# Cross-attention: the products with the values, from one head at a time on 128 output rows to four heads side by side on 32 rows each, a group of four heads in one go

## The reference, cut to what matters

```
q = (x @ Wq).reshape(b, n, 32, 16)            # b = 4 batches, n = 512 queries, 32 heads of 16
k, v = jnp.split(ctx @ Wkv, 2, axis=-1)       # 512 keys
q, k = apply_axial_rope(q, pos), apply_axial_rope(k, pos)
logits = jnp.einsum('bqhd,bkhd->bhqk', q, k) * scale
w = jax.nn.softmax(logits, axis=-1)
attn = jnp.einsum('bhqk,bkhd->bqhd', w, v)
return attn.reshape(b, n, 512) @ Wout + bout
```

## Time and profile before

| | |
|---|---|
| median of 3 runs | 6926.31 us (6921.14 to 6929.72) |
| profiled execution | 6916.92 us, its span 6915.1 us |
| first score matmul of the stage | 5753.1 us from the span's start |
| last copy out of `out_ps` begins | 6535.2 us |
| PE, DVE, ACT, POOL busy over the span | 82%, 62%, 40%, 25% |

### The profile page before, as it was taken

One profiled execution on the slowest core, in us unless ns is written; L12 is line 12 of the kernel. 1 busy time (PEld: TensorE's weight loads), 2 busy tenths in 40 slices (PEclk: granted clock), 3 DMA queues, 4 the chain that ended last, 5 costly groups with the idle time before them and its releaser, 6 DMA issues. The chain is left out here.

```text
span 6915.1 us, 91344 instructions
## 1 busy us (share of the span) xinstructions
PE 5668.5 (82%) x29317; PEld 3875.2 (56%) x29317; DVE 4276.0 (62%) x7058; ACT 2762.2 (40%) x5087; POOL 1762.9 (25%) x1756
## 2 busy tenths in 40 slices
PE   4889338996788888888888888888888777999946
PEld 3656225563466666666666666666666534555523
DVE  4777663223377777777667677767776445666566
ACT  4555111110244444444444444444444224666512
POOL 2556000202133333333333333333333141000100
PEclk8999659998799999999999999999999898999978
DMA  1011004344200001000001100000000021111110
GB/s 53 25 25 25 18 18 185 125 153 142 86 28 26 26 26 35 26 26 26 26 26 40 29 24 28 26 26 24 27 26 22 1 75 61 44 43 43 34 50 24
DMA packets 261461, 307.07 MB, mean 44 GB/s; under 512 B 27840, under 2 KB 180928, under 8 KB 259808
## 3 DMA queue, kind: packets, MB, share of 16 engines
q1 hardware_dynamic: 247120, 248.43, 11.8%
q0 software_dynamic: 13984, 54.01, 2.2%
HBM read 245.88 MB, written 56.49 MB: 44 GB/s over the span
## 5 line engine op out<-in xcount | busy, mean ns | idle before, releaser
L1647 POOL TENSOR_TENSOR delta_rule_suffix<-delta_rule_suffix,delta_rule_prefix 128x256 f32<-128x256 f32 x448 | 496.2, 1108 | 1780.3 <-ACT delta_rule_prefix L1703 1174.8
L1956 PE MATMUL delta_rule_level<-delta_rule_qk_second,delta_rule_k_first 128*128 128x128 f32 x3072 | 427.1, 283 | 142.8 <-DVE delta_rule_L_large L1768 126.0
L1956 PEld LDWEIGHTS delta_rule_level<-delta_rule_qk_second,delta_rule_k_first 128*128 128x128 f32 x3072 | 385.6, 195 | 193.9 <-DVE delta_rule_qk_second L1776 142.0
L2398 PE MATMUL attend_out_ps<-attend_probsT,attend_v_head 128*128 128x512 f32 x1024 | 481.5, 593 | 0.0
L1929 PE MATMUL delta_rule_proj<-delta_rule_hT,delta_rule_w_qkv 128*128 128x512 f32 x1024 | 474.4, 607 | 0.0
L1638 POOL TENSOR_TENSOR delta_rule_k_first<-delta_rule_qk,delta_rule_suffix 128x256 f32<-128x256 f32 x384 | 306.4, 798 | 627.8 <-PE delta_rule_level L1944 494.4
L2425 DVE TENSOR_REDUCE attend_top<-attend_scores 128x1 f32<-128x512 f32 x512 | 328.5, 684 | 159.2 <-PE attend_scores L2380 159.1
L472 DVE TENSOR_TENSOR_SCAN scan_hs<-scan_decay,scan_inp 128x512 f32<-128x512 f32 x256 | 307.9, 1216 | 189.6 <-PE scan_inp L534 91.3
L309 POOL TENSOR_TENSOR scan_hc<-scan_hs,scan_c_rows 128x512 f32<-128x512 f32 x256 | 333.1, 1308 | 272.5 <-DVE scan_hs L472 253.3
L1864 DVE TENSOR_TENSOR delta_rule_X<-delta_rule_X,delta_rule_inv 128x512 f32<-128x512 f32 x384 | 262.3, 683 | 199.8 <-PE delta_rule_inv L1985 199.8
L1776 DVE TENSOR_TENSOR delta_rule_qk_second<-delta_rule_qk,delta_rule_prefix 128x512 f32<-128x512 f32 x448 | 339.9, 759 | 48.8 <-issue 14.0
(11 more groups left out here) (466 smaller groups left out, 12893.7 us busy)
## 6 DMA issues: line engine op xcount, KB each, us to landing
moe_w_d<-in_w_down SPq DMA_DIRECT2D x39, 512.0 KB, 4.3
scan_c_rows<-bc_dram SPq DMA_DIRECT2D x64, 256.0 KB, 3.7
delta_rule_w_qkv<-in_kda_wq SPq DMA_DIRECT2D x64, 256.0 KB
delta_rule_w_qkv<-in_kda_wk SPq DMA_DIRECT2D x64, 256.0 KB
delta_rule_w_qkv<-in_kda_wv SPq DMA_DIRECT2D x64, 256.0 KB
delta_rule_inv_beta<-beta_dram SPq DMA_DIRECT2D x64, 256.0 KB
delta_rule_w_o<-in_kda_wo SPq DMA_DIRECT2D x64, 256.0 KB, 4.5
parts_dram<-qkv_parts POOLq DMA_DIRECT2D x24, 512.0 KB, 6.1
```

The source lines that it names most:

```text
L1647: pool.tensor_tensor(first, first, whole_second, ALU.mult).then_inc(suffix_done, 1)
L1956: last = pe.matmul(level_ps[(i + 1) % 2][:, c, :], left, qk_second[:, i % 2, :, c * CHUNK // 2:(c + 1) * CHUNK // 2], start=True, stop=True)
L2398: last = pe.matmul(out_ps[:], v_head[:, j, i, :], probsT[:, j % 2, i, :], start=(j == 0 and i == 0), stop=(j == H - 1 and i == TPB - 1))
```

## The change

The eight heads of a tile form two halves (GROUP = 4), half 0 for steps j = 0 to 3 and half 1 for steps 4 to 7. `head(j)` says which head step j works on: 0, 2, 4, 6 in the first half and 1, 3, 5, 7 in the second. The stationary operand `v_head[:, j, i, :]` is now 32 columns wide (COLS), 16 with values and 16 zeros, and the output of head q of a half goes to rows 32q to 32q + 31 of `out_ps`. The two halves add up in the same rows. `probsT` keeps all eight heads instead of two, 64 KB a partition instead of 16 KB. `v_head` shrinks from 16 KB to 4 KB a partition.

The products of a half are issued in one run of 16 program matmuls, i = 0 to 3 outside and q = 0 to 3 inside, between turn 1 and turn 2 of one head step: of step 5 for half 0 of the same tile, of step 1 for half 1 of the tile before. Their number is the same as before, 512, and the moving operand is still 128x512. The last half stands bare at the end. `weighed` counts halves now. DVE and ACT wait for it ahead of the first write to a `probsT` slot; DVE's copy of `out_ps` moves from step 0 to step 3.

```
+    GROUP = 4
+    WEIGH_AT = 1
+    COLS = 2 * X_DIM
+    def head(j):
+        return 2 * (j % GROUP) + j // GROUP
...
-        v_head = sc.sb("v_head", [P, H, TPB, P])
+        v_head = sc.sb("v_head", [P, H, TPB, COLS])
-        probsT = sc.sb("probsT", [P, 2, TPB, S])
+        probsT = sc.sb("probsT", [P, H, TPB, S])
...
-                def weigh(n, j, i):
-                    m = n * H + j
+                def weigh(n, half, i):
+                    m = n * H + half * GROUP + GROUP - 1
                     pe.wait_ge((even_copied, odd_copied)[i % 2], 2 * m + i // 2 + 1)
                     if i == 0:
                         pe.wait_ge(v_ready, m + 1)
-                        if j == 0:
+                        if half == 0:
                             pe.wait_ge(out_copied, n)
-                    last = pe.matmul(out_ps[:], v_head[:, j, i, :], probsT[:, j % 2, i, :],
-                                     start=(j == 0 and i == 0), stop=(j == H - 1 and i == TPB - 1))
+                    for q in range(GROUP):
+                        j = half * GROUP + q
+                        last = pe.matmul(out_ps[q * COLS:(q + 1) * COLS, :], v_head[:, j, i, :], probsT[:, j, i, :],
+                                         start=(half == 0 and i == 0), stop=(half == 1 and i == TPB - 1))
...
                     for i in range(TPB):
                         turn(n, j, i)
-                        if i % 2 == 1 and not first:
-                            weigh(*before, i - 1)
-                            weigh(*before, i)
+                        if i == WEIGH_AT and j % GROUP == 1:
+                            for part in range(TPB):
+                                if j >= GROUP:
+                                    weigh(n, 0, part)
+                                elif not first_tile:
+                                    weigh(n - 1, 1, part)
                     if last:
                         for i in range(TPB):
-                            weigh(n, j, i)
+                            weigh(n, 1, i)
...
                         if i % 2 == 1:
                             dve.wait_ge(probs_turned, TPB * m + i + 1)
-                            dve.tensor_copy(probsT[:, j % 2, i, :], turned[1][:].rearrange("p a b -> p (a b)")).then_inc(odd_copied, 1)
+                            if i == 1:
+                                dve.wait_ge(weighed, 2 * n + j // GROUP + 1)
+                            dve.tensor_copy(probsT[:, j, i, :], turned[1][:].rearrange("p a b -> p (a b)")).then_inc(odd_copied, 1)
...
-                    if j == 0 and not first:
+                    if j == GROUP - 1 and not first_tile:
                         copy_out(n - 1)
```

More of the change, by code:

```diff
@@ L2326, in steps @@
             for j in range(H):
-                step(0, j, j == 0, False)
+                step(0, j, j == 0, False, True)
             with engine.Fori(1, N - 1) as n:
                 for j in range(H):
-                    step(n, j, False, False)
+                    step(n, j, False, False, False)
             for j in range(H):
-                step(N - 1, j, False, j == H - 1)
+                step(N - 1, j, False, j == H - 1, False)
         with nc.Block() as block:
@@ L2339, in _ @@
                 sp.sem_inc(exp_done, TPB)
-                sp.sem_inc(weighed, H)
+                sp.sem_inc(weighed, 2)
                 sp.sem_inc(sums_copied, 2)
@@ L2345, in _ @@
                         s = j % RING
-                        at = slice(j * X_DIM, (j + 1) * X_DIM)
+                        at = slice(head(j) * X_DIM, (head(j) + 1) * X_DIM)
                         sp.wait_ge(scores_done, TPB * (n * H + j + 1))
@@ L2365, in _ @@
                     for j in range(H):
-                        at = slice(j * X_DIM, (j + 1) * X_DIM)
-                        pool.wait_ge(weighed, n * H + j + 1)
-                        pool.tensor_copy(v_head[:, j, :, at], v_flat[:, n, :, at]).then_inc(v_ready, 1)
+                        at = slice(head(j) * X_DIM, (head(j) + 1) * X_DIM)
+                        to = slice(j // GROUP * X_DIM, (j // GROUP + 1) * X_DIM)
+                        pool.wait_ge(weighed, n * 2 + j // GROUP + 1)
+                        pool.tensor_copy(v_head[:, j, :, to], v_flat[:, n, :, at]).then_inc(v_ready, 1)
                 pool.wait_ge(bout_loaded, 16)
@@ L2395, in weigh, with step @@
                         pe.wait_ge(v_ready, m + 1)
-                        if j == 0:
+                        if half == 0:
                             pe.wait_ge(out_copied, n)
-                    last = pe.matmul(out_ps[:], v_head[:, j, i, :], probsT[:, j % 2, i, :],
-                                     start=(j == 0 and i == 0), stop=(j == H - 1 and i == TPB - 1))
+                    for q in range(GROUP):
+                        j = half * GROUP + q
+                        last = pe.matmul(out_ps[q * COLS:(q + 1) * COLS, :], v_head[:, j, i, :], probsT[:, j, i, :],
+                                         start=(half == 0 and i == 0), stop=(half == 1 and i == TPB - 1))
                     if i == TPB - 1:
                         last.then_inc(weighed, 1)
-                def step(n, j, first, last):
-                    before = (n, j - 1) if j else (n - 1, H - 1)
+                def step(n, j, first, last, first_tile):
                     if first:
@@ L2427, in copy_out, with step @@
                 def copy_out(n):
-                    dve.wait_ge(weighed, H + (n + 1) * H)
+                    dve.wait_ge(weighed, 2 + (n + 1) * 2)
                     dve.tensor_copy(out_flat[:, n, :], out_ps[:]).then_inc(out_copied, 1)
-                def step(n, j, first, last):
+                def step(n, j, first, last, first_tile):
                     m = n * H + j
@@ L2467, in step @@
                             act.wait_ge(probs_turned, TPB * m + i + 1)
-                            act.activation(probsT[:, j % 2, i, :], turned[0][:].rearrange("p a b -> p (a b)"),
+                            if i == 0:
+                                act.wait_ge(weighed, 2 * n + j // GROUP + 1)
+                            act.activation(probsT[:, j, i, :], turned[0][:].rearrange("p a b -> p (a b)"),
                                            ACT.Copy).then_inc(even_copied, 1)
```

2 lines of the change are left out of this document (1 added, 1 removed).

## The result

The changed kernel takes 6844.18 us (median of 4 runs, 6840.94 to 6848.36) against 6926.35 (4 runs, 6921.14 to 6929.72) for the kernel before: a ratio of 0.9887, 95% interval 0.9874 to 0.9899. That is 82.2 us less (the interval allows 70 to 87), where 48 more was forecast.

What follows compares the result with a forecast made beforehand. The prediction took a full PE to bound the stage, 6.04 us a head, 773 us. Head steps 602, bursts 208, last burst 7.7 and start 3 made 821, so 48 more: 6974 us, range 6840 to 7025.

Steps and rivals of the forecast that it cites:

- W: Length of one burst of 16 program matmuls on PE, taken as 7.7 us with only neighbouring strips overlapping.
- The narrow and wide rows: Profile rows of the kernel before where 16-column records stand 0.43 us apart on their own strip, between wide matmuls.
- the rival: All four strips run at once, burst 3.6 us, the SP queue then decides: 6843 us, chance 0.25.
- the bounds of 3.6 and 14.0: Limits on the burst's length in us: all four strips at once, or no overlap.
- The cap: SP queue's transfers allow no lasting head rate under 5.39 us, so the change gives at most 83 us.
- A head step without products, 4.7: Closed chain of ACT and PE for one head when no products are issued, taken as 4.7 us.
- The delay, W - 1.0: Time a burst between turn 1 and turn 2 adds to the chain: 1.0 us hidden, 6.7 added.
- the forecast's own sum: Stage time from head steps 602, bursts inside steps 208, last burst 7.7 and start 3: 821 us against 773.
- Break-even at W of about 6.2: Burst length in us at which the changed kernel would take as long as the kernel before.
- The edits costed at nothing: DVE's moved copy of `out_ps`, the two added waits on `weighed` and POOL's copies were to cost nothing.
- The sign that the prediction gave for the queue: In steps without a burst, ACT's even copies 5.4 us apart with SP never waiting would mean the queue bounds them.
- The clock's rival: PE, no longer full, loses its full granted clock for part of the time: 46 us more, 7020 us, chance 0.08.

Runs made afterwards that it cites:

- s9: Changed kernel, cross-attention layer alone, with key loads moved to GpSimd's queue and GpSimd's 16 additions spread one to a tile: 1044.01 us.
- The wide burst: Changed kernel, cross-attention layer alone, products regrouped but kept on 128 output columns instead of narrow strips: 1372.75 us.
- s11: Kernel before the change, cross-attention layer alone, with key loads moved from SP's to GpSimd's queue: 1149.57 us.
- s2: Changed kernel with the five other phases left out, cross-attention layer alone: 1057.95 us.
- s10: Changed kernel, cross-attention layer alone, with products spread over four steps, key loads on GpSimd's queue and additions one to a tile: 980.17 us.
- f12: Whole changed kernel, all phases, with spread products, key loads on GpSimd and additions one to a tile: 6760.86 us, ratio 0.9771 to the kernel before.
- s7: Changed kernel, cross-attention layer alone, with key loads moved to GpSimd's queue, the 16 additions still in one piece: 1062.55 us.
- s8: Changed kernel, cross-attention layer alone, with products spread over four steps and key loads on GpSimd's queue, additions in one piece: 982.64 us.

## Why the prediction was wrong

**The step that failed** is W, the length of the burst, 7.7 us in the sum and 3.57 in the trace. The step is in the part on the burst: "If matmuls start in program order, strip 1's first starts beside strip 0's second, not before it. So only neighbours pair up: 16 program matmuls take 17 slots". The trace has 8 slots. A second record that waits for its strip doesn't hold back the next strip; up to three may wait (W = 3.61, 6.21 and 8.79 for four, six and eight records in a row). The narrow and wide rows have only one strip, so they bear on what a strip does with its own records and not on its neighbour; the text took the second for granted from the first. It also gave "no row shows PE starting a matmul ahead of another" as weight against the rival, which is the absence of any two strips in the trace, not evidence. Between the bounds of 3.6 and 14.0 the case was open, and the chance of 0.25 for full overlap was too low.

**What bounds the kernel before.** Right: PE was full, and with PE's work cut the stage became 75.4 us shorter. The cap that it put on the gain, 83 us by the SP queue, held.

**A head step without products, 4.7.** Right: 4.68.

**The delay, W - 1.0.** Right in kind: it is 2.76 for W = 3.57, so 0.8 is hidden. The working took products to begin 0.24 behind ACT's first copy; it is 6115.90 - 6115.57 = 0.33. It took 0.64 from the turn to the copy, which is 6120.16 - 6119.47 = 0.69, and 1.87 between the copies without products, which is 1.82 in s9: 1.82 - 0.33 - 0.69 = 0.8. The wide burst adds 239 us of 243 expected. With the measured W the forecast's own sum reads 128 x 4.68 + 31 x 2.76 + 3.6 + 3 = 691, 82 under 773. The medians differ by 82.2; the stage in the traces by 75.4, and the slow tiles, which the sum has only as 3 us at the start, account for most of the rest. So W is the one term that was wrong by enough to turn the forecast.

**Break-even at W of about 6.2.** Right within 3 us of 1134: W = 6.21 gave 1136.78, and 48.45 us a tile against 48.39 before.

**The edits costed at nothing.** `out_ps`'s copy in step 3 and the waits for `weighed` cost under 0.1 us a step: outside the burst no step in the loop of s9 is longer than 4.76 (622.02 to 626.78).

**The rival's mechanism.** Its time was right, and its reason by half. It let the SP queue decide, 4 x 5.39 = 21.6 us, with the chain at 21.4 behind it. The chain measures 21.57. With the queue eased (s9) it alone holds the stage at 43.16 us a tile, and the whole gain is 14 us of 1058; so both limits are met, the queue's in some tiles and the chain's in most. This case's two bounds lie closer together than the 0.2 us to which they were worked out. The sign that the prediction gave for the queue, steps without a burst 5.4 apart, would have misled: the steps are 4.68 apart and the queue still never waits, because a step with a burst is long enough for it to catch up, with loads four heads ahead.

**The clock.** 0.98 to 1.00, with PE at 78 of 100 us, where the stage ahead has 0.87 and 0.85 at 64. The clock's rival did not come up.

## What to carry to other kernels

Where four outputs fit on 32 rows each, put their matmuls side by side with not more than two float32 matmuls of one strip in a row: 32 records then take the time of 8, and one or two in a row made no difference (3.57 and 3.61 us). Before a change takes 20% from the full engine, work out the next two limits to 0.1 us; here a chain and a queue stood equal behind it, easing one showed little, and both together, with GpSimd's additions spread, took the gain from 82 to 159 us. Work that is made short should be cut to pieces that each fit into a gap: a burst fills one gap, four pieces fill four.

## What the runs showed of the hardware

**Strips.** A float32 matmul on 32 columns is two records on the same strip, and four strips run at once. Up to three records may wait behind the running one of a strip without holding back the strip behind it in the program; the fourth holds it. A narrow burst takes 0.13 to 0.2 us beside its slots, and the wide one nothing; that this is the turn to narrow strips and back is argued, not tested by itself.

**VectorE and GpSimd.** A 128x4 copy between SBUF tensors, 160 ns at the median, took 19.63 us while GpSimd ran 16 additions back to back, 18.2 in s11 and 4.5 in s2; with one addition to a tile the longest is 0.6 in s9 and 1.69 in s10 and f12. In s7 and s10 it ends 0.03 to 0.04 us behind an addition. The Trainium skill, "SBUF — State Buffer", section "SBUF: two separate sides", has a port pair that VectorE's faster copies and GpSimd share, held by one for a whole instruction. A copy that ends with an addition agrees with that. A stall over all 16 instructions, and in s10 one of a copy that had begun 0.37 us ahead of the addition, do not follow from it. No run here shows that it is this port, and why a copy is held for 4.5 us in s2 and for 19.6 in s7 stays open.

**Queues.** SP issues six of these transfers in 5.4 us. GpSimd's issue of three, in s7:

```profile
906.70 1.83 POOL L2378 DMA_DIRECT2D attend_k_stack<-parts_dram  x3 [2.13 <-PE attend_scores L2403]
```

They take 1.83 us beside SP's three, and PE waits for no transfer between 400 and 800 us of s8, at 4.9 us a head.
